# Output products one step earlier in PE's queue of the first feed-forward

## The chip, the cores and the metric

The kernel runs on one core of one Trainium2 chip. The metric is device time in microseconds, the median of several executions; lower is better. The profile shows one execution of its own. Engines: PE (TensorE) multiplies, ACT (ScalarE) and DVE (VectorE) read PE's results from the eight accumulator banks `ps`, POOL (GpSimd) works between SBUF tiles, SP issues most transfers.

## The reference

Two layers over 2048 tokens of width 128, each of them an attention and a feed-forward with eight experts, of which each token takes two. The change touches the feed-forward of the first layer:

```python
x = x + _L0_xattn_ref(_layernorm(x), ctx_1024, ctx_1024, ...)
x = x + _L0_ffn_ref(_layernorm(x), L0_ffn_w_gate, L0_ffn_w_g, L0_ffn_w_u, L0_ffn_w_d)
x = x + _L1_xattn_ref(_layernorm(x), ctx_1024, ctx_1024, ...)
x = x + _L1_ffn_ref(_layernorm(x), L1_ffn_gate_w, ...)

def _L0_ffn_ref(x, w_gate, w_g, w_u, w_d):      # D = 128, M = 176, E = 8, K = 2
    scores = x @ w_gate
    topk_scores, topk_idx = jax.lax.top_k(scores, K)
    topk_probs = jax.nn.softmax(topk_scores, axis=-1)
    gating = jnp.sum(jax.nn.one_hot(topk_idx, E) * topk_probs[..., None], axis=-2)
    hidden = jax.nn.silu(jnp.einsum('bsd,edm->ebsm', x, w_g)) * jnp.einsum('bsd,edm->ebsm', x, w_u)
    expert_out = jnp.einsum('ebsm,emd->ebsd', hidden, w_d)
    return jnp.einsum('bse,ebsd->bsd', gating, expert_out)
```

## The kernel before

Every engine has a program of its own, written out by hand in the order in which the engine issues it; semaphores join them. The stages are: loading and keys, values and queries of layer 0, attention 0, routing, the first feed-forward (`experts0` on each engine), and then the same for layer 1 with its own feed-forward (`experts1`).

A product in better than float16 precision is three products of a high and a low float16 part (helper `three`, lines 963 to 965: high by high, high by low, low by high). All products of the two feed-forwards have these three lines in the trace; the tile names tell them apart: `ps<-area,wg` and `ps<-area,wu` are gate and up, `ps<-wd,area` are the output products.

The first feed-forward treats the eight experts' hidden rows, 8 x 176 = 1408, as 11 blocks of 128 (STEPS0), and the tokens as four groups of 512. It has two halves (`i`), each with two groups: 22 steps (K0) in a half. Step k, n over both halves:

- PE, `gate_up(n)` (line 1191): six products of 512 columns, three for gate into bank k % 2 and three for up into bank 2 + k % 2. It waits until DVE has finished step n - 2 (semaphore `gt`), because the banks are reused. The first two steps of each half are issued ahead: those of half one in `routing`, those of half two in the tail of half one (line 1213).
- PE, line 1212: one product of 512 columns that spreads the tokens' expert weights over the hidden rows, into bank 4 + k % 2. It increments `up`.
- ACT, line 407: Silu of the gate bank, after `up`. Then, in ACT's queue, line 413: the float16 copy (`hid`, high part) of the step before, k - 1, after `gt` of that step. In four steps of a half (CHUNK_STEPS 2, 7, 12, 17) line 418 follows, a conversion of later weights.
- DVE, line 835: up times Silu; line 841: times the spread expert weights, into `gated`; it increments `gt`. DVE also makes the low parts of the later weights (line 847) and, after step 15, adds the first group's result to x with new statistics (`residual0`, lines 857 to 577); that of the second group comes after step 21.
- POOL, line 554: the low part of `hid`, `gated` minus the float16 copy; it increments `lo`. After step 16 POOL has the statistics of the first group as well (lines 495 and 498).
- PE, `down` (line 1172): twelve products of 128 columns, `hid` by the output weights, accumulated over the 11 steps of a group into bank 6 or 7. It waits for `lo` of its step. LAG0 = 3: it is issued three steps behind.

`hid`, `gated` and `act_f` have four buffers each.

Of the kernel before, what the change touches and what calls it, by code (L numbers as in the profile page):

```python
# [31 lines left out]
P = 128  # L32
# [14 lines left out]
STEPS0 = HID0 // P  # L47
# [9 lines left out]
def positive_wait(eng, sem, value):  # L57

    if not isinstance(value, int) or value > 0:
        eng.wait_ge(sem, value)  # L60


def build(nc, a, out):
# [5 lines left out]
    with ExitStack() as ctx:  # L69
        def sb(name, shape, dt):  # L70
            return ctx.enter_context(nc.sbuf_tensor(name, shape, dt))

        def sems(names, suffix=""):
            return {n: ctx.enter_context(nc.semaphore(n + suffix)) for n in names.split()}
# [46 lines left out]
        wd = sb("wd", [P, 2, HID0], F16)  # L121
# [11 lines left out]
        def carve(shape, dt):  # L133
            n = int(np.prod(shape)) * (4 if dt == F32 else 2) // 4
            ap = area[:, used[0]:used[0] + n]
            used[0] += n
            assert used[0] <= 12400, used
            if dt != F32:
                ap = ap.bitcast(dt)
            names = "abcd"[:len(shape)]  # L140
            if len(shape) > 1:
                ap = ap.rearrange(f"p ({' '.join(names)}) -> p {' '.join(names)}", **dict(zip(names[1:], shape[1:])))
            return ap
# [18 lines left out]
        hid = carve([4, 2, GT], F16)  # L162
# [16 lines left out]
        ps = ctx.enter_context(nc.psum_tensor("ps", [P, 8, 512], F32))  # L179
# [11 lines left out]
        F = [sems("xh xd xt_ps xt_hi xt_lo lg_ps lg top idx ex pr oh cb c16 ct_ps ct_a ct_d "  # L191
                  "up act hi lo down res " + ("t1 gt", "b1 b2_ps b2_r")[l], f"_f{l}") for l in range(2)]
# [767 lines left out]
        def _(pe):  # L960
            def three(dst, lhs, rhs, start=True, stop=True, **kw):

                pe.matmul(dst, lhs[0], rhs[0], start=start, stop=False, **kw)  # L963
                pe.matmul(dst, lhs[0], rhs[1], start=False, stop=False, **kw)  # L964
                return pe.matmul(dst, lhs[1], rhs[0], start=False, stop=stop, **kw)  # L965
# [208 lines left out]
            def down(dst, h, w, first, last):  # L1174


                for t in range(G):
                    r = slice(t * P, (t + 1) * P)
                    mm = three(dst[:, r], (h[:, 0, r], h[:, 1, r]), w, start=first and t == 0, stop=last, skip_group_check=True)
                return mm  # L1180

            K0 = 2 * STEPS0
            LAG0 = 3

            def place0(n):
                i, k = divmod(n, K0)
                f = slice((k % STEPS0) * P, (k % STEPS0 + 1) * P)
                tok = slice(1024 * i + GT * (k // STEPS0), 1024 * i + GT * (k // STEPS0) + GT)
                return i, k, f, tok

            def gate_up(n):

                i, k, f, tok = place0(n)
                xs = (xTa[:, 0, tok], xTa[:, 1, tok])
                positive_wait(pe, F[0]["gt"], n - 1)
                three(ps[:, k % 2, :], (wg[:, 0, f], wg[:, 1, f]), xs)
                three(ps[:, 2 + k % 2, :], (wu[:, 0, f], wu[:, 1, f]), xs)

            def experts0():
                q = F[0]  # L1200
                pe.wait_ge(q["ct_d"], 1)
                for i in range(GROUPS // 2):
                    for k in range(K0 + LAG0):
                        n = K0 * i + k
                        if k < K0:
                            _, _, f, tok = place0(n)
                            if k >= 2:
                                gate_up(n)
                            if n == K0:
                                pe.wait_ge(q["ct_a"], 1)  # L1210
                            positive_wait(pe, q["gt"], n - 1)
                            pe.matmul(ps[:, 4 + k % 2, :], expert_rows[:, f], combT[:, tok], start=True, stop=True).then_inc(q["up"], 1)  # L1212
                        elif i == 0 and k < K0 + 2:
                            gate_up(n)
                        if k >= LAG0:
                            j = k - LAG0
                            pe.wait_ge(q["lo"], K0 * i + (j + 1))
                            if j == 0:
                                pe.wait_ge(q["res"], 2 * i + 1)
                            half, f = divmod(j, STEPS0)  # L1220
                            down(ps[:, 6 + half, :], hid[:, j % 4, :, :],
                                 (wd[:, 0, f * P:(f + 1) * P], wd[:, 1, f * P:(f + 1) * P]), f == 0, f == STEPS0 - 1).then_inc(q["down"], 1)

            K1 = GROUPS * STEPS1
            LAG1 = 3
# [62 lines left out]
            attention(0)  # L1288
            routing(0)
            experts0()  # L1290
            for g in range(GROUPS):
                project_keys(1, g)
# [40 lines left out]
```

## Time and profile before

| | us |
|---|---|
| median of 3 runs (lowest, highest) | 533.04 (532.51, 534.41) |
| the profiled execution's own time | 533.98 |
| its span, first to last instruction | 531.8 |
| the first feed-forward on PE, from its first product of line 1212 to its last output product | 137.6 to 243.8 |
| PE busy in the span | 464.0 (87%) |
| DVE, ACT, POOL busy | 386.5, 368.3, 191.5 |
| mean granted clock of TensorE | 0.91 |

Shares of the whole span are means over stages with different limits, so the feed-forward is to be read from its own stretch. A granted clock of 1.00 is the 2.4 GHz level, 0.50 is 1.2 GHz; a value between them is a stretch with both. PE's matmuls overlap: a record lasts longer (0.38 us for 512 columns, 0.22 for 128) than the distance to the next start (0.215 and 0.056), so the beat is read from starts. In the rows, a time in brackets is the idle time of the engine before the instruction and what ended it. A step's number isn't printed; it is counted from the starts of line 1212, one in each step.

### The profile page before, as it was taken

What the parts mean: (1) busy time and instruction counts of PE and PEld (TensorE: products, weight loads), DVE (VectorE), ACT (ScalarE), POOL (GpSimd) and SP (SyncE); (2) the same over time, 40 slices, a digit from 0 to 9 for tenths busy, and PEclk for the clock granted to TensorE, in tenths of its full rate; (3) what the DMA queues carried; (4) which work ended last, traced back from release to release, by engine and by line L of the source; (5) the groups of instructions that cost most, each with busy time, mean ns of one, the idle gap of its engine ahead of it and who ended that gap; (6) DMA issues with size and microseconds to landing.
All of it is one profiled execution on the core that took longest, in us unless ns stands there. A gap on an engine that the chain in (4) does not pass through costs nothing.

```text
span 531.8 us, 15145 instructions
## 1 busy us (share of the span) xinstructions
PE 464.0 (87%) x5467; PEld 313.3 (59%) x5467; DVE 386.5 (73%) x1006; ACT 368.3 (69%) x675; POOL 191.5 (36%) x285
## 2 busy tenths in 40 slices
PE   5669888875899979994969999669999999999996
PEld 3445656553366536653636666537777777777775
DVE  6765888878587857784636999878767676676765
ACT  3555676771455536553837878548999999999995
POOL 7921576771155545566503887510000000000000
PEclk9895698995799989998867999859999999999999
DMA  7292000000012101100130000000000000000002
GB/s 188 49 280 54 2 3 1 3 2 1 0 41 76 46 2 39 41 1 9 19 56 1 3 4 1 4 1 2 1 2 1 0 0 0 0 0 0 0 21 59
DMA packets 18952, 13.47 MB, mean 25 GB/s; under 512 B 1682, under 2 KB 17236, under 8 KB 18900
## 3 DMA queue, kind: packets, MB, share of 16 engines
q1 hardware_dynamic: 18840, 12.75, 9.3%
q8 instruction: 34, 0.56, 0.5%
q14 instruction: 18, 0.15, 0.1%
q10 hardware_dynamic: 60, 0.02, 0.0%
HBM read 9.61 MB, written 1.05 MB: 20 GB/s over the span
## 4 chain that ended last, share of the span: by engine, by line
PE 58%; issue 12%; DVE 12%; POOL 9%; ACT 6%; DMA 1%; SPq 1%; POOLq 0%; DVEq 0%; ACTq 0%
PE ps L963 15%; PE ps L965 14%; PE ps L964 14%; POOL area L554 5%; PE ps L1117 4%; PE ps L1049 3%; DVE area L739 2%; PE ps L1076 2%; ACT vals L316 1%; PE ps L1007 1%; PE ps L1025 1%; DVE area L715 1%; POOL rstd L498 1%; POOL area L519 1%; DVE stats L573 1%
## 5 line engine op out<-in xcount | busy, mean ns | idle before, releaser
L892 DVE TENSOR_TENSOR area<-area 128x512 f16<-128x512 f32 x128 | 87.9, 689 | 46.4 <-ACT area L436 45.9
L963 PE MATMUL ps<-w,area 128*128 (+1 forms) x512 | 92.3, 219 | 0.5 <-DVE area L892 0.5
L964 PE MATMUL ps<-w,area 128*128 (+1 forms) x512 | 92.3, 219 | 0.0
L965 PE MATMUL ps<-w,area 128*128 (+1 forms) x512 | 92.3, 219 | 0.0
L432 ACT ACTIVATE area<-ps,b_now 128x512 f32<-128x512 f32 x128 | 87.7, 685 | 2.9 <-ACT b_now L426 1.3
L436 ACT ACTIVATE area<-area 128x512 f16<-128x512 f32 x128 | 80.6, 630 | 4.1
L554 POOL TENSOR_TENSOR area<-area 128x512 f16<-128x512 f32 x44 | 51.0, 1159 | 54.8 <-ACT area L413 54.8
L963 PEld LDWEIGHTS ps<-w,area 128*128 128x128 f16 x512 | 50.1, 98 | 15.3 <-DVE area L892 1.2
L964 PEld LDWEIGHTS ps<-w,area 128*128 128x128 f16 x512 | 50.1, 98 | 14.2
L739 DVE TENSOR_REDUCE area<-ps 128x8 f32<-128x512 f32 x64 | 41.2, 685 | 19.6 <-PE ps L1117 19.6
L407 ACT ACTIVATE area<-ps 128x512 f32<-128x512 f32 x44 | 26.0, 597 | 40.2 <-PE ps L1212 39.7
L965 PEld LDWEIGHTS ps<-w,area 128*128 128x128 f16 x512 | 50.1, 98 | 0.0
L963 PE MATMUL ps<-area,w 128*128 128x512 f16 x128 | 49.2, 385 | 0.8 <-DVE area L799 0.8
L964 PE MATMUL ps<-area,w 128*128 128x512 f16 x128 | 49.3, 385 | 0.0
L965 PE MATMUL ps<-area,w 128*128 128x512 f16 x128 | 49.3, 385 | 0.0
L1049 PE MATMUL ps<-ident,area 128*128 128x128 f32 x256 | 44.3, 323 | 0.2 <-ACT area L364 0.2
L835 DVE SCALAR_TENSOR_TENSOR area<-ps,area 128x512 f32<-128x512 f32 x44 | 30.2, 685 | 18.9 <-ACT area L407 18.7
L1117 PE MATMUL ps<-keys,q_T 32*64 32x256 f16 x768 | 39.5, 314 | 2.9 <-DVE q_T L673 1.6
L534 POOL TENSOR_TENSOR area<-area 128x512 f16<-128x512 f32 x32 | 41.4, 1293 | 0.1
L364 ACT ACTIVATE area<-ps 128x512 f32<-128x512 f32 x64 | 34.7, 594 | 5.6 <-PE ps L1076 4.6
L913 DVE SCALAR_TENSOR_TENSOR x_res<-ps,area,x_res 128x128 f32<-128x128 f32 x128 | 35.8, 343 | 0.9 <-PE ps L965 0.9
L1049 PEld LDWEIGHTS ps<-ident,area 128*128 128x128 f32 x256 | 33.6, 165 | 3.9 <-ACT area L364 1.8
(185 smaller groups left out, 1171.9 us busy)
## 6 DMA issues: line engine op xcount, KB each, us to landing
w_stage<-in_L_ffn_W SPq DMA_DIRECT2D x8, 512.0 KB, 4.1
keys<-area SPq DMA_DIRECT2D x32, 48.0 KB
area<-in_ctx SPq DMA_DIRECT2D x4, 256.0 KB, 4.0
x_res<-in_x SPq DMA_DIRECT2D x4, 256.0 KB, 5.3
out<-x_res SPq DMA_DIRECT2D x4, 256.0 KB, 2.3
w<-in_L_ffn_w_g SPq DMA_DIRECT2D x1, 704.0 KB, 4.5
w<-in_L_ffn_w_u SPq DMA_DIRECT2D x1, 704.0 KB, 6.3
w<-in_L_ffn_w_d SPq DMA_DIRECT2D x1, 704.0 KB, 8.2
```

The source lines that it names most:

```text
L432: nc.scalar.activation(act_f[:, k % 4, :], ps[:, k % 4, :], ACT.Gelu, bias=b1_now[:, k % STEPS1:k % STEPS1 + 1], scale=1 / WSCALE).then_in ...
L436: nc.scalar.activation(hid[:, k % 4, 0, :], act_f[:, k % 4, :], ACT.Copy).then_inc(q["hi"], 1)
L534: nc.gpsimd.tensor_tensor(pT[:, (t + 1) % 2, 1, 4:8, :].rearrange("p a b -> p (a b)"), p_f[:, (t + 1) % 2, :], pT[:, (t + 1) % 2, 0, 4:8, ...
L554: nc.gpsimd.tensor_tensor(hid[:, k % 4, 1, :], gated[:, k % 4, :], hid[:, k % 4, 0, :], ALU.subtract).then_inc(q["lo"], 1)
L739: nc.vector.tensor_reduce(mx[:, v, h * hh:(h + 1) * hh], ps[:, 2 * v + h, :].rearrange("p (h k) -> p h k", k=SEQ), axis=AX.X, op=ALU.max). ...
L892: nc.vector.tensor_tensor(hid[:, k % 4, 1, :], act_f[:, k % 4, :], hid[:, k % 4, 0, :], ALU.subtract).then_inc(q["lo"], 1)
L913: ins = nc.vector.scalar_tensor_tensor(x[:, G * g + t, :], ps[:, 4 + g % 2, t * P:(t + 1) * P], comb[:, G * g + t, bass.ds(e, 1)], x[:, G ...
L963: pe.matmul(dst, lhs[0], rhs[0], start=start, stop=False, **kw)
L964: pe.matmul(dst, lhs[0], rhs[1], start=False, stop=False, **kw)
L965: return pe.matmul(dst, lhs[1], rhs[0], start=False, stop=stop, **kw)
L1049: mm = pe.transpose(ps[:, 4 + h, n * P:(n + 1) * P], probs[:, (t + 1) % 2, c:c + P], ident[:, :])
L1117: mm = pe.matmul(ps[64 * b:64 * b + 64, 2 * v + n // 2, HALF // 2 * odd:HALF // 2 * (odd + 1)].rearrange("p (j k) -> p j k", j=QUAD), q_T[ ...
```

## The change

The output products become a function, `put_down(i, j)`, with the same waits in the same order and the same products. In steps 3 to 21 of a half it is called at the beginning of the step, ahead of `gate_up(n)` and of line 1212, and no longer behind them. In the three last turns (k from 22 to 24) `gate_up` of the next half is still issued first. LAG0 stays 3, and no other engine's program is changed.

```diff
@@ experts0 of PE
                         if k < K0:
                             _, _, f, tok = place0(n)
+                            if k >= LAG0:
+                                put_down(i, k - LAG0)
                             if k >= 2:
                                 gate_up(n)
                             if n == K0:
                                 pe.wait_ge(q["ct_a"], 1)
                             positive_wait(pe, q["gt"], n - 1)
                             pe.matmul(ps[:, 4 + k % 2, :], expert_rows[:, f], combT[:, tok], start=True, stop=True).then_inc(q["up"], 1)
-                        elif i == 0 and k < K0 + 2:
-                            gate_up(n)
-                        if k >= LAG0:
-                            j = k - LAG0
-                            pe.wait_ge(q["lo"], K0 * i + (j + 1))
-                            if j == 0:
-                                pe.wait_ge(q["res"], 2 * i + 1)
-                            half, f = divmod(j, STEPS0)
-                            down(ps[:, 6 + half, :], hid[:, j % 4, :, :],
-                                 (wd[:, 0, f * P:(f + 1) * P], wd[:, 1, f * P:(f + 1) * P]), f == 0, f == STEPS0 - 1).then_inc(q["down"], 1)
+                        else:
+                            if i == 0 and k < K0 + 2:
+                                gate_up(n)
+                            put_down(i, k - LAG0)
+
+            def put_down(i, j):
+
+                q = F[0]
+                pe.wait_ge(q["lo"], K0 * i + (j + 1))
+                if j == 0:
+                    pe.wait_ge(q["res"], 2 * i + 1)
+                half, f = divmod(j, STEPS0)
+                down(ps[:, 6 + half, :], hid[:, j % 4, :, :],
+                     (wd[:, 0, f * P:(f + 1) * P], wd[:, 1, f * P:(f + 1) * P]), f == 0, f == STEPS0 - 1).then_inc(q["down"], 1)
```

## Rows read from the trace of the kernel before

**Rows 1.** The stretches: us, each engine's busy us (instructions), TensorE clock, DMA share, GB/s.

```profile
203.00:225.00 22.00, 22.00 (x193) 13.62 (x192) 16.70 (x25) 13.05 (x22) 11.78 (x11) 1.00 0.16 48
```

**Rows 2.** The waits of 137 to 246 us: who waited for whom, us, times, longest.

```profile
PE ps L963 <- DVE area L841: 6.7, 4, 3.5
...
PE ps L963 <- POOL area L554: 1.9, 2, 1.1
```

**Rows 3.** The timeline, steps 10 to 12 of half two: start, us, engine.

```profile
214.28 0.22 PE L963 MATMUL ps<-wd,area 128*128 128x128 f16 x1
...
214.95 0.38 PE L963 MATMUL ps<-area,wg 128*128 128x512 f16 x1
...
216.25 0.38 PE L1212 MATMUL ps<-area,expert_rows 128*128 128x512 f16 x1
...
216.46 0.22 PE L963 MATMUL ps<-wd,area 128*128 128x128 f16 x1
...
217.16 0.62 ACT L413 ACTIVATE area<-area 128x512 f16<-128x512 f32 x1
...
217.85 1.16 POOL L554 TENSOR_TENSOR area<-area 128x512 f16<-128x512 f32 x1 [1.02 <-ACT area L413]
...
218.02 0.69 DVE L841 TENSOR_TENSOR area<-ps,area 128x512 f32<-128x512 f32 x1
...
218.43 0.38 PE L1212 MATMUL ps<-area,expert_rows 128*128 128x512 f16 x1
```

**Rows 4.** The timeline, end of half two: POOL's end and the products waiting for it.

```profile
240.37 1.16 POOL L554 TENSOR_TENSOR area<-area 128x512 f16<-128x512 f32 x1 [1.02 <-ACT area L413]
...
241.58 0.23 PE L963 MATMUL ps<-wd,area 128*128 128x128 f16 x1 [1.10 <-POOL area L554]
...
243.17 0.23 PE L963 MATMUL ps<-wd,area 128*128 128x128 f16 x1 [0.75 <-POOL area L554]
...
243.85 0.38 PE L963 MATMUL ps<-ctx_T,wT 128*128 128x512 f16 x1
```

**Rows 5.** The timeline, start of half one, steps 2 to 5.

```profile
142.81 0.59 PE L1212 MATMUL ps<-area,expert_rows 128*128 128x512 f16 x1
...
144.62 1.16 POOL L554 TENSOR_TENSOR area<-area 128x512 f16<-128x512 f32 x1 [2.51 <-ACT area L413]
...
149.07 0.38 PE L1212 MATMUL ps<-area,expert_rows 128*128 128x512 f16 x1
```

**Rows 6.** The timeline, steps 15 to 21 of half one, with the first residual.

```profile
170.88 0.38 PE L1212 MATMUL ps<-area,expert_rows 128*128 128x512 f16 x1
...
176.08 0.69 DVE L841 TENSOR_TENSOR area<-ps,area 128x512 f32<-128x512 f32 x1
...
177.51 1.16 POOL L554 TENSOR_TENSOR area<-area 128x512 f16<-128x512 f32 x1 [1.69 <-ACT area L413]
...
178.13 0.38 PE L1212 MATMUL ps<-area,expert_rows 128*128 128x512 f16 x1
...
180.22 1.16 POOL L554 TENSOR_TENSOR area<-area 128x512 f16<-128x512 f32 x1
```

**Rows 7.** The timeline, step 21 and the end of half one.

```profile
184.68 0.38 PE L1212 MATMUL ps<-area,expert_rows 128*128 128x512 f16 x1
...
187.88 1.16 POOL L554 TENSOR_TENSOR area<-area 128x512 f16<-128x512 f32 x1 [0.44 <-ACT area L413]
...
190.16 0.59 PE L1212 MATMUL ps<-area,expert_rows 128*128 128x512 f16 x2
```

**Rows 8.** The timeline, start of half two, steps 2 and 3.

```profile
196.74 0.63 PE L1212 MATMUL ps<-area,expert_rows 128*128 128x512 f16 x1
...
198.80 0.38 PE L1212 MATMUL ps<-area,expert_rows 128*128 128x512 f16 x1
```

**Rows 9.** The stretches in the two attention stages (columns as in Rows 1).

```profile
80.00:90.00 10.00, 8.76 (x131) 6.00 (x130) 7.98 (x22) 6.89 (x15) 6.87 (x12) 0.83 0.01 2
290.00:300.00 10.00, 9.36 (x157) 6.10 (x160) 9.20 (x28) 7.91 (x19) 7.75 (x15) 1.00 0.01 2
```

## Prediction

> **Names.** Step k is one of the 22 steps of a half (44 in the first feed-forward). G(k) are its six gate and up products (512 columns each), C(k) the product that spreads the expert weights, D(k) its twelve output products (128 columns each). S(k) is ACT's Silu, M(k) DVE's last multiplication, H(k) ACT's float16 copy, L(k) POOL's subtraction (L554), which D(k) waits for. Times "C(k) + 2.76" count from the start of C(k).
>
> **What bounds the kernel now.** I read first the stretches, to see which engine is full in the feed-forward: from 203 to 225 us PE is busy 22.00 of 22.00 us at a granted clock of 1.00, the 2.4 GHz level, while DVE, ACT and POOL are at 16.70, 13.05 and 11.78 [rows 1]. Second the waits: in the whole feed-forward the output products wait for POOL twice only, 1.9 us, and the gate products for DVE four times, 6.7 us [rows 2]. So POOL's result is always there in time, but for the end. The chain of waits names POOL L554 step after step here; that is how it walks back through ACT and PE's queue, and the full PE speaks against it. Third the timeline, for the beat: C(11) starts at 216.25 and C(12) at 218.43, 2.18 us apart [rows 3]. That is PE's own work: 214.28 to 214.95 for D (0.67), then to 216.25 for G (1.30), then 0.21 for C, 2.18 in all. PE issues without a hole.
>
> **The change, part by part.** No instruction is added or removed, and no DMA, SP, ACT, DVE or POOL instruction moves. In PE's queue each group C(k), D(k-3), G(k+1) becomes C(k), D(k-2), G(k+1): between two G the output products are those of one step later. So the real edit is a lag of 2 in place of 3, and D's wait is now in front of G(k+1), C(k+1) and all behind them, and through C(k+1) in front of S, M, H and L of that step.
>
> *When L is ready.* With C(11) at 216.25, H(10) starts at 217.16 (it is queued behind S(11), which needs C(11)), L(10) runs 217.85 to 219.01 [rows 3]. So L(k-1) ends at C(k) + 2.76. M(11) ends at 218.71, C(11) + 2.46, before ACT comes to H(11) a beat later (217.16 + 2.18 = 219.34): M is not the late one. Before, D(k-1) is reached after C(k+2), at C(k) + 4.57, 1.8 us after L; that is the cover. After, it is reached after C(k+1), at C(k) + 2.18 + 0.21 = 2.39, and L is 0.37 us late.
>
> *What a waiting D costs.* At the end of half two L ends at 240.37 + 1.16 = 241.53 and the waiting product starts at 241.58: 0.05 from one to the other. A D that has waited takes 243.17 to 243.85, 0.68 [rows 4], then 1.30 for G: 1.98 to the next C.
>
> *The loop.* C(k+2) = C(k) + 2.76 + 0.05 + 1.98 = C(k) + 4.79, in place of 2 x 2.18 = 4.36. One wait of 0.43 in every two steps (or smaller ones that come to it), since a late C(k+2) pushes its own S, H and L, and gives the D in between its time back: 0.215 us a step. From step 5 to 15 of each half that is 10 x 0.215 = **2.15 us**, twice. The bounds: with no cost on restarting (0.05 and 0.01 left out) 4.73, or 0.185 a step; with ACT's hand-over to POOL, 217.16 + 0.62 = 217.78 to 217.85, 0.07 in place of 0.05 [rows 3], 0.225. A wait of 0.42 in every step, 2.60 a beat, is excluded, as the D in between finds its L ready. I take the row that shows the very wait.
>
> *The start of half one.* C(2) stands at 142.81 as before; C(2) takes 0.43 at the low clock; D(0) is ready, so it goes in at 143.24, and C(3) comes at 143.24 + 0.67 + 1.30 = 145.21. L(1) ends at 144.62 + 1.16 = 145.78 [rows 5], so D(1) at 145.83, C(4) at 147.81. L(2) ends at C(3) + 2.76 = 147.97, D(2) at 148.02, C(5) at 150.00 against 149.07: **+0.93**, of which 0.67 is only the D done earlier. *Of half two:* C(2) at 196.74 at a low clock; D(0) behind it, half of it at the low level (0.33 more): C(3) at 196.74 + 0.43 + 1.00 + 1.30 = 199.47, in place of 198.80 [rows 8]. In half one L(1) ends 144.62 + 1.16 - 142.81 = 2.97 after C(2) [rows 5]; here that is 199.71, D(1) at 199.76 and C(4) at 201.74. L(2) ends at 199.47 + 2.76 = 202.23, so D(2) at 202.28, C(5) at 204.26. Before it is 216.25 - 6 x 2.18 = 203.17 [rows 3]: **+1.09**. A low stretch can end elsewhere: 0.7 either way.
>
> *Steps 15 to 21, with the first residual on DVE.* Before, M(16) ends at 176.77, C(15) + 5.89, as DVE does the residual first; that makes PE wait and puts C(18) at 178.13, C(15) + 7.25, of which 0.71 is over three beats [rows 6]. The loop's own three steps come to about 7.19, so the new wait hides in the old one: C(18) at +7.25 to 7.39. After that L(16), 177.51 to 178.67, M(16) + 1.90, gives D(16) at +7.84 and C(19) at +9.82. L(17) stands behind POOL's own statistics, starts at 180.22 and ends at 181.38, M(16) + 4.61 [rows 6], so D(17) starts at +10.55 and C(20) at +12.53; D(18) is ready when reached, C(21) at +14.71. Before: 184.68 - 170.88 = 13.80 [rows 6, 7]. **+0.91**, in each half.
>
> *The end of a half.* The tail keeps its order, with one D less in it (D(18) is done). In half one before, C(22) starts at 190.16, C(21) + 5.48, all PE work. After, PE would be 0.67 earlier, but L(21) ends at 187.88 + 1.16 = 189.04, C(21) + 4.36 [rows 7]; D(21) starts at +4.41, C(22) 0.68 later at +5.09, or +5.12 with a small wait of G for M(21): **-0.36**. In half two D(21) waits for L(21) before and after: **0**, and nothing is paid back.
>
> *Sum.* Half one 0.93 + 2.15 + 0.91 - 0.36 = 3.63, half two 1.09 + 2.15 + 0.91 = 4.15: +7.8 us. Nothing later hides it: DVE's second residual, POOL's normalisation and the key transfers all start from the end of half two. Against the profiled run: 531.8 + 7.8 = 539.6 of span, with the 2.2 around it 541.8. The median of the runs shown, 533.04, is 0.94 below the profiled run, 533.98. I forecast **540.8**.
>
> **Rivals.** *Not slower.* The loop decides at one point: L(k-1) has to end by C(k) + 2.34, and it ends at 2.76. If the rows put PE's starts 0.4 too early against POOL's (matmul ends are modelled), or H went ahead of S, there is no wait, and what is left are gains: the early D fills PE's wait of 0.71 at the residual in both halves, and 0.36 at the tail: 533.0 - 1.8 = 531.3. For it: the margin is a sixth of a beat. Against it: the 0.05 between POOL and PE is read from the same two clocks, and the two waits at the end of half two are real ones [rows 4]. Chance 0.05.
>
> *The clock falls.* PE, full until now, gets a hole in every second step. In the first attention, where PE waits for others, a stretch has 8.76 of 10 us busy and a granted clock of 0.83 (a part of it at the 1.2 GHz level), but in the second one 9.36 busy goes with 1.00 [rows 9]; after the change PE would be busy about 91%. At 0.83 a pair of steps is 4.36 / 0.83 = 5.25 of PE work, 0.46 over the 4.79 of the forecast; over the 16 pairs of steps 5 to 21 of both halves that is +7.4, 548.2. Chance 0.06.
> The Trainium skill ("TensorE: Matmul & The Clock Gate", A second HAM failure mode: psum-queue depth-cycling) says that frequent micro-idles between groups of matmuls can make the clock go to and fro between its levels; by it the result would be this rival. The row of the second attention stage disagrees, that of the first fits.
>
> *Something unseen*: 0.04.
>
> **How the numbers follow.** The forecast has 0.85. Its own bounds: 0.03 less a step or 0.01 more, over 32 steps, is -1.0 or +0.3; the starts 0.7 each; the low stretches of the later stages, which can fall elsewhere when all is 7.8 us later, 1.5. Not all go one way: 538.0 to 544.0. The rivals at 531.3 and 548.2 stay outside with 0.11. A measurement of this kernel tells some 0.5% (2.7 us) from no change: slower by more 0.94, within 0.03, faster by more 0.03 (a gain of 1.8 is still "within").
>
> **What the profile would show.** The waits of the feed-forward should have a new large group, PE's output products for POOL L554, about 16 to 25 times at some 0.26 each (0.21 + 0.43 after the start of C, less the 0.38 that C's record lasts), while PE's wait for DVE before step 18 goes to near nothing. The starts of C should be about 2.4 apart on average, uneven (2.18 and 2.6), POOL's subtractions as well, all durations unchanged, the granted clock 1.00 in the steady stretches. The feed-forward should end near 251.6 in place of 243.85, and what follows keep its length. Even beats of 2.18 would prove the first rival, a clock under 1.00 in a steady stretch the second. I am wrong in size if ACT turns H ahead of S, or if the starts of the halves hide more than I think.

## The result, and the profile after

| | before | after |
|---|---|---|
| median of 5 runs, us (lowest, highest) | 533.91 (532.51, 534.41) | 540.63 (539.67, 541.84) |
| the profiled execution's own time | 533.98 | 539.67 |
| its span | 531.8 | 537.5 |
| PE from its first product of the first feed-forward (C(0)) to the first product behind it | 137.56 to 243.85 = 106.3 | 138.98 to 252.09 = 113.1 |

The ratio of after to before is 1.0134, 95% interval 1.0113 to 1.0155: 6.7 us slower. The forecast was 540.8.

The waits of after, from 137 to 254 us (who waited for whom, us in total, times, longest), answer to [rows 2]:

```profile
PEld ps L963 <- POOL area L554: 23.3, 40, 1.5
...
PE ps L963 <- DVE area L841: 5.6, 2, 3.5
...
PE ps L963 <- POOL area L554: 5.2, 15, 1.3
```

PE's output products now wait for POOL, and not only at the end: 15 times with 5.2 us, of which the two waits at the end of half two are 1.34 and 0.75. That leaves 13 of 0.24 each. The row of the weight loads (PEld), 40 times against 2 before, shows that nearly every D has to wait; many of these waits don't appear on the matmul row, because the record of C lasts 0.38 us and covers them. The wait for DVE went from four times to two: the two of 0.5 us at the residual are off the matmul row. The large ones, up to 3.5 us at the starts of the halves, are still there.

The timeline of after, steps 7 to 10 of half two (start, us, engine), answers to [rows 3]:

```profile
216.43 0.62 ACT L413 ACTIVATE area<-area 128x512 f16<-128x512 f32 x1
...
217.13 1.16 POOL L554 TENSOR_TENSOR area<-area 128x512 f16<-128x512 f32 x1 [1.26 <-ACT area L413]
...
217.90 0.38 PE L1214 MATMUL ps<-area,expert_rows 128*128 128x512 f16 x1
...
218.34 0.23 PE L963 MATMUL ps<-wd,area 128*128 128x128 f16 x1
...
219.02 0.38 PE L963 MATMUL ps<-area,wg 128*128 128x512 f16 x1
...
219.51 1.16 POOL L554 TENSOR_TENSOR area<-area 128x512 f16<-128x512 f32 x1 [1.22 <-ACT area L413]
...
220.32 0.38 PE L1214 MATMUL ps<-area,expert_rows 128*128 128x512 f16 x1
...
220.72 0.23 PE L963 MATMUL ps<-wd,area 128*128 128x128 f16 x1
```

H(7) at 216.43 and L(7) from 217.13 to 218.29 stand behind S(8), as before. But D(7) is now what PE has next after C(9), at 217.90 + 0.21 = 218.11, and it starts at 218.34, 0.05 after the end of L(7). G(10) follows at 219.02, C(10) at 220.32. One beat later D(8) has its turn at 220.53 and starts at 220.72, again 0.05 after L(8) (219.51 + 1.16 = 220.67). Two steps take 4.80 us. In half two the wait is spread over both steps (2.42 and 2.38), in half one it falls mostly on every other (2.57 and 2.22). The sum is the same.

The clock, in stretches of the steady part of each half (columns as in [rows 1]):

```profile
149.00:173.00 24.00, 22.89 (x194) 12.74 (x191) 16.73 (x25) 13.07 (x23) 11.58 (x10) 1.00 0.15 46
...
203.00:225.00 22.00, 21.59 (x175) 11.64 (x173) 15.96 (x23) 11.60 (x20) 10.84 (x10) 1.00 0.17 48
```

It is 1.00 in both, so the holes did not bring it down. PE is busy 22.89 of 24 us by its records, which cover part of each hole; the holes themselves are 0.44 in 4.80.

### The profile page after: what moved, and what is told of

Read it like the earlier page. It is cut to its first block, busy times and chain, and to the rows that moved or that the text cites. A ratio compares the mean times of both kernels' runs of the same rounds, so it can differ in the third digit from the quotient of the medians.

```text
span 537.5 us, 15145 instructions
## 1 busy us (share of the span) xinstructions
PE 465.6 (87%) x5467; PEld 309.5 (58%) x5467; DVE 388.9 (72%) x1006; ACT 368.6 (69%) x675; POOL 191.1 (36%) x285
## 3 DMA queue, kind: packets, MB, share of 16 engines
HBM read 9.61 MB, written 1.05 MB: 20 GB/s over the span
## 4 chain that ended last, share of the span: by engine, by line
PE 50%; issue 19%; POOL 12%; DVE 11%; ACT 5%; DMA 1%; SPq 1%; POOLq 1%; DVEq 0%; ACTq 0%
PE ps L963 12%; PE ps L965 12%; PE ps L964 12%; POOL area L554 8%; PE ps L1117 4%; PE ps L1049 3%; DVE area L739 2%; PE ps L1076 2%; ACT vals L316 1%; PE ps L1025 1%; DVE area L715 1%; PE ps L1007 1%; POOL rstd L498 1%; DVE stats L573 1%; DMA x_res<-in_x 1%
## 5 line engine op out<-in xcount | busy, mean ns | idle before, releaser
L963 PE MATMUL ps<-wd,area 128*128 128x128 f16 x176 | 32.3, 222 | 5.9 <-POOL area L554 5.2
```

## The steps of the forecast, one by one

From the starts of C in both profiles (of each pair the second is after), us:

| stretch | half one | difference, forecast | half two | difference, forecast |
|---|---|---|---|---|
| C(0) to C(2) | 5.25, 4.02 | -1.23, 0 | 6.58, 6.66 | +0.08, 0 |
| C(2) to C(5) | 6.26, 7.36 | +1.10, +0.93 | 6.42, 7.43 | +1.01, +1.09 |
| C(5) to C(15) | 21.81, 24.00 | +2.19, +2.15 | 21.81, 23.98 | +2.17, +2.15 |
| C(15) to C(21) | 13.80, 14.69 | +0.89, +0.91 | 13.79, 14.70 | +0.91, +0.91 |
| C(21) to the next stretch | 5.48, 5.17 | -0.31, -0.36 | 5.09, 5.10 | +0.01, 0 |

The last row of half two ends at the first product behind the feed-forward. The sum is +6.8, or +8.05 without the first cell; the forecast was +7.8. Outside the feed-forward, what stands before it was 1.4 longer in this execution and what stands behind it 2.5 shorter.

The first cell isn't the change's doing. C(0) to C(2) takes 5.25 us in six of the fourteen kernels profiled here and 4.02 in the other eight, in both orders, and C(2) itself starts at 142.81 before and 143.00 after. The +1.10 beside it is also made up otherwise than the forecast had it. It took D(0) to be ready behind C(2); but L(0) ended at 142.38 + 1.15 = 143.53, and D(0) waited for it, to 143.59. In the run with a lag of two (below), where C(0) to C(2) is 5.25 as before, C(2) to C(5) takes 7.19 us, +0.93, as reckoned.

Two rows need their lines. Steps 15 to 18 of half one, which answer to [rows 6] (C(15), M(16), C(18)):

```profile
174.36 0.38 PE L1214 MATMUL ps<-area,expert_rows 128*128 128x512 f16 x1
...
179.55 0.69 DVE L841 TENSOR_TENSOR area<-ps,area 128x512 f32<-128x512 f32 x1
...
181.61 0.38 PE L1214 MATMUL ps<-area,expert_rows 128*128 128x512 f16 x1
```

C(15) to C(18) is 7.25 as before: M(16) still ends 5.88 after C(15) and sets G(18). What the loop costs in these three steps hides in the wait for M(16), and the whole +0.9 of the stretch comes behind C(18), from the waits of D(16) and D(17). The end of half one, which answers to [rows 7]:

```profile
189.05 0.38 PE L1214 MATMUL ps<-area,expert_rows 128*128 128x512 f16 x1
...
191.57 0.39 PE L963 MATMUL ps<-area,wg 128*128 128x512 f16 x1
...
192.26 1.15 POOL L554 TENSOR_TENSOR area<-area 128x512 f16<-128x512 f32 x1 [0.43 <-ACT area L413]
...
194.22 0.59 PE L1214 MATMUL ps<-area,expert_rows 128*128 128x512 f16 x2
```

C(21) starts at 189.05, G(23) at 191.57, and C(22) with C(23) at 194.22, 5.17 later. L(21) ends at 192.26 + 1.15 = 193.41, while PE comes to D(21) only at 191.57 + 1.30 + 0.67 = 193.54 (G(23), D(20)). So the tail is not set by L(21), which the forecast made its first bound (5.09), but by M(21), which ends at C(21) + 2.46 = 191.51 and lets G(23) begin. The forecast had that as "a small wait of G for M(21)", 5.12.

## The experiments

Each was compared with the kernel before, run beside it on the same chip (medians 533.92, 533.96 and 533.64 for the three groups of four). Stretches are read from the starts of C in the profile, as above.

**One half only.** In half one the order of the change, in half two that of before.

```diff
-                            if k >= LAG0:
+                            if k >= LAG0 and i == 0:
                                 put_down(i, k - LAG0)
                             if k >= 2:
                                 gate_up(n)
...
                             pe.matmul(ps[:, 4 + k % 2, :], ...).then_inc(q["up"], 1)
+                            if k >= LAG0 and i == 1:
+                                put_down(i, k - LAG0)
```

> The output products stand ahead of the gate products in half one only; half two has the order of before. Theory (a loop of 4.79 us for two steps instead of 4.36, and the prices of the starts, the residual and the tails): half one costs 3.6 us and half two nothing, 537.5 us against 533.9 of before, ratio 1.0068. In the profile the steps 5 to 15 take 24.0 us in half one and 21.8 in half two. Rival (the clock, or anything that concerns the whole program, makes the difference): the two halves look alike, or the later stages differ, and the time lies near 534 or near 541.

Measured: 538.82 us, ratio 1.0086 (1.0056 to 1.0115). The profiled execution has C(5) and C(15) of half one, then of half two, at

```profile
151.93 0.38 PE L1214 MATMUL ps<-area,expert_rows 128*128 128x512 f16 x1
...
175.92 0.38 PE L1214 MATMUL ps<-area,expert_rows 128*128 128x512 f16 x1
...
208.75 0.38 PE L1214 MATMUL ps<-area,expert_rows 128*128 128x512 f16 x1
...
230.56 0.38 PE L1214 MATMUL ps<-area,expert_rows 128*128 128x512 f16 x1
```

so 23.99 us in half one and 21.81 in half two. The residual stretch is 14.70 and 13.79. The loss goes with the order, half by half; nothing that concerns the whole program explains it. The time is 4.9 us over before, 1.3 more than forecast; the forecast ratio, 1.0068, is inside the interval, and both 1 and the 1.0134 of the change are outside.

**A lag of two, in the place of before.** The one line of LAG0 in the kernel before.

```diff
-            LAG0 = 3
+            LAG0 = 2
```

> The order of before, with LAG0 at 2 instead of 3: C(k), D(k-2), G(k+1), with D still written behind G and C of its step. Theory (the change is nothing but a lag of 2): the steps 5 to 15 take 24.0 us in both halves, C every 2.4 us on average, and the time is that of the changed kernel within 1 us, 540 to 541.5 us, ratio 1.012 to 1.015. Rival (the place ahead of G matters by itself, as the weights for G can't be loaded while D waits): D now waits in the same place of the stream, so this rival would have to give something else than the changed kernel, and under 1.005 if the lag were harmless.

Measured: 540.58 us, ratio 1.0126 (1.0067 to 1.0184), beside 540.63 of the changed kernel. Steps 5 to 15 take 24.00 and 23.99 us, 15 to 21 14.70 and 14.69. The timeline of half two (start, us, engine):

```profile
212.17 0.38 PE L1212 MATMUL ps<-area,expert_rows 128*128 128x512 f16 x1
...
212.81 0.23 PE L963 MATMUL ps<-wd,area 128*128 128x128 f16 x1 [0.26 <-POOL area L554]
...
213.78 1.16 POOL L554 TENSOR_TENSOR area<-area 128x512 f16<-128x512 f32 x1 [1.02 <-ACT area L413]
...
214.79 0.38 PE L1212 MATMUL ps<-area,expert_rows 128*128 128x512 f16 x1
```

C(k) at 212.17, C(k+1) at 214.79, 2.62 later, and then 2.18; D starts at 212.81, not at 212.38. Written as a move ahead of the gate products, the change is a shorter lag. In the steps of a half both kernels give PE the same row of products, so this run shows that the two are one change. It can't show whether the place of the wait ahead of G costs anything by itself; the next run and the one with a shorter L do that, as they keep the place and take the wait away.

**High part first, in the changed order.** The wait for L stands before the last four products of D.

```diff
+            def down_high_first(dst, h, w, first, last, j):
+                for t in range(G):
+                    r = slice(t * P, (t + 1) * P)
+                    pe.matmul(dst[:, r], h[:, 0, r], w[0], start=first and t == 0, stop=False, ...)
+                    pe.matmul(dst[:, r], h[:, 0, r], w[1], start=False, stop=False, ...)
+                pe.wait_ge(F[0]["lo"], j)
+                for t in range(G):
+                    r = slice(t * P, (t + 1) * P)
+                    mm = pe.matmul(dst[:, r], h[:, 1, r], w[0], start=False, stop=last, ...)
+                return mm
...
-                pe.wait_ge(q["lo"], K0 * i + (j + 1))
+                pe.wait_ge(q["hi"], K0 * i + (j + 1))
...
-                down(ps[:, 6 + half, :], ...
+                down_high_first(ps[:, 6 + half, :], ...
```

> The changed kernel, with D in two parts: the eight products with the high part of hid first, behind a wait for ACT's copy H only, then the wait for POOL's L and the four products with the low part. L is needed 8 x 0.056 = 0.45 us later, 2.84 after C instead of 2.39, and it is there at 2.81. Theory (the loss is L coming 0.42 us too late and nothing else): C every 2.18 us in the steady steps, steps 5 to 15 take 21.8 us; what is left is the start of each half (+0.67), D(17) behind POOL's statistics (+0.46) and a gain at the tails (-0.6 and -0.45): 535 us, ratio 1.002. Rival (holes or the order on PE itself, or the clock): it stays at 1.010 or more.

Measured: 534.36 us, ratio 1.0012 (0.9981 to 1.0044). Steps 5 to 15 take 21.81 us in both halves. L of POOL, C, the first product of D, the first with the low part (four in one row), the next C:

```profile
210.77 1.16 POOL L554 TENSOR_TENSOR area<-area 128x512 f16<-128x512 f32 x1 [1.02 <-ACT area L413]
...
211.34 0.38 PE L1226 MATMUL ps<-area,expert_rows 128*128 128x512 f16 x1
...
211.56 0.22 PE L1186 MATMUL ps<-wd,area 128*128 128x128 f16 x1
...
212.00 0.39 PE L1191 MATMUL ps<-wd,area 128*128 128x128 f16 x4
...
213.52 0.38 PE L1226 MATMUL ps<-area,expert_rows 128*128 128x512 f16 x1
```

L ends at 211.93, 0.37 too late for the first product of D at 211.56, and 0.07 ahead of the first product with the low part at 212.00. The beat is 2.18 again. The instructions are the same on all engines; D alone has its products in two parts and its wait between them, and the loss in the steady steps is gone: the cause is that L comes late, and by how much. What is left is in part as forecast: 15 to 21 takes 14.26 (L(17) behind POOL's statistics, +0.46), and the end of half two 4.64 in place of 5.09 (-0.45). C(2) to C(5) is +0.28 and +1.05, where +0.67 each was expected. The tail of half one missed: 5.16, 0.3 shorter than before and not 0.6. With L out of the way, this shows again that M(21) sets it. C(15) to C(18) is still 7.25.

**High part first, in the order of before.** The same edit of D in the kernel before.

> Control of the run before: the order of before, with D in the same two parts. Theory: L is 1.8 us early in every step, so the steady steps stay at 2.18; only the last D of half two, which waits for L, is 0.45 us shorter: 533.5 us, ratio 0.999. Rival (the two parts gain or cost something by themselves, for instance at the loading of weights): a ratio under 0.996 or over 1.004 here, by which the run before would have to be read anew.

Measured: 534.52 us, ratio 0.9996 (0.9964 to 1.0027); all steady stretches as before, 21.81 and 13.80, and the end of half two 4.65 in place of 5.09, as expected. In the time of the whole kernel the edit has neither a price nor a gain that could be measured.

**A longer L, both orders.** One subtraction of 192 columns more, ahead of L.

```diff
                     pool.wait_ge(q["hi"], n + 1)
+                    nc.gpsimd.tensor_tensor(hid[:, k % 4, 1, 0:192], gated[:, k % 4, 0:192],
+                                            hid[:, k % 4, 0, 0:192], ALU.subtract).then_inc(q["pd"], 1)
+                    pool.wait_ge(q["pd"], n + 1)
                     nc.gpsimd.tensor_tensor(hid[:, k % 4, 1, :], gated[:, k % 4, :], hid[:, k % 4, 0, :],
                                             ALU.subtract).then_inc(q["lo"], 1)
```

> The order of before, with one more POOL subtraction of 192 columns ahead of each L (192 of its 512 columns are done twice), which L waits for: L ends about 0.6 us later, at C + 3.4. Theory (in the order of before D has 1.8 us of cover): the steady steps stay at 2.18 us, only the tails lose, 0.2 in half one and 0.6 in half two: 534.7 us, ratio 1.0015. Rival (POOL's pace or its traffic costs time by itself): over 1.005.

> The changed order with the same 0.6 us more ahead of L. Theory (two steps take L's latency + 0.05 + 1.98): 4.79 + 0.6 = 5.4 us for two steps, 2.7 a step in place of 2.4, so that steps 5 to 15 take 27 us in place of 24; with the starts, the residual part and the tails about 12 us more than the changed kernel: 552.5 us, ratio to before 1.035. Rival (the wait is paid in every step): 0.6 a step, 44 steps, 26 us more, 566 us. Rival (POOL's result isn't what D waits for): no more than with the order of before.

Measured in the order of before: 537.48 us, ratio 1.0065 (1.0034 to 1.0097). The ten steady steps lose only 0.21 and 0.29 us for ten times 0.62 of longer L: the cover of 1.8 us holds. The forecast of the total missed, and by its number the rival (over 1.005) came true. In the profile the feed-forward loses 4.5 us from C(2) on. Some 2.7 of it, in steps 15 to 21 and in the tails, is L coming late where its cover is thin. The first such place is D(17), behind POOL's statistics (the two POOL rows are the added piece and L(17)):

```profile
182.28 1.09 POOL L554 TENSOR_TENSOR area<-area 128x192 f16<-128x192 f32 x1
...
183.45 1.16 POOL L557 TENSOR_TENSOR area<-area 128x512 f16<-128x512 f32 x1
...
184.66 0.23 PE L966 MATMUL ps<-wd,area 128*128 128x128 f16 x1 [0.56 <-POOL area L557]
```

L(17) ends at 184.61 and D(17) waits 0.56; the added piece took 1.09 here, not 0.55. Steps 15 to 21 take 14.56 in place of 13.80, in both halves, the tails 0.4 and 0.8 more, C(2) to C(5) 0.6 and 0.7. I had put 0.2 and 0.6 on the tails and nothing on the two other places.

The rest, in the steady steps and the starts, goes with the rival, a price of POOL's work by itself. DVE's conversion of later weights in step 7 of half one, in the kernel before:

```profile
156.16 0.69 DVE L847 SCALAR_TENSOR_TENSOR w<-w_stage,w 128x512 f32 x1 [0.27 <-ACT w L418]
```

and here, with L(6) ahead of it:

```profile
156.67 1.16 POOL L557 TENSOR_TENSOR area<-area 128x512 f16<-128x512 f32 x1
...
157.16 1.21 DVE L850 SCALAR_TENSOR_TENSOR w<-w_stage,w 128x512 f32 x1 [0.27 <-ACT w L418]
```

The conversion takes 1.21 in place of 0.69 where POOL's subtraction runs into it, up to 157.83, and ends 0.54 behind it. DVE's next multiplications come late by it, and the beats from C(9) and C(14) are 2.27 and not 2.18. At the start of half one a conversion takes 1.27, and PE waits 0.46 us for DVE at 148.75, in the beat from C(4).

In the order of the change: 557.3 us, ratio 1.0431 (1.0385 to 1.0478). Steps 5 to 15 take 27.12 us in both halves, 5.42 for two steps. The added piece, L, C, D, the next C:

```profile
220.12 0.55 POOL L554 TENSOR_TENSOR area<-area 128x192 f16<-128x192 f32 x1 [1.27 <-ACT area L413]
...
220.74 1.15 POOL L557 TENSOR_TENSOR area<-area 128x512 f16<-128x512 f32 x1
...
220.88 0.38 PE L1217 MATMUL ps<-area,expert_rows 128*128 128x512 f16 x1
...
221.95 0.23 PE L966 MATMUL ps<-wd,area 128*128 128x128 f16 x1 [0.70 <-POOL area L557]
...
223.93 0.38 PE L1217 MATMUL ps<-area,expert_rows 128*128 128x512 f16 x1
```

L starts 0.62 later (220.12 to 220.74), and D starts 0.06 after its end (221.89 to 221.95). 4.79 + 0.62 = 5.41 against 5.42: the formula of the loop, with its slope of one half a step, and not the rival's 0.6 in every step, which would be 3.0 a step where 2.71 is measured. Steps 15 to 21 take 16.93 in place of 14.70, and from C(2) to the first product behind the feed-forward it is 13.0 us more than in the changed kernel, where about 12 was expected. The total is 4.8 over its forecast, which lies outside the interval (1.035 for 1.0385 to 1.0478). The profile doesn't show the rest: the execution that was profiled took 553.26 us, 0.8 over the forecast, and was the fastest of four; why the other three took 556.4 to 558.3 stays open.

**A shorter L, in the changed order.**

```diff
+                    c = GT if k < 4 else GT // 2
-                    nc.gpsimd.tensor_tensor(hid[:, k % 4, 1, :], gated[:, k % 4, :], hid[:, k % 4, 0, :],
+                    nc.gpsimd.tensor_tensor(hid[:, k % 4, 1, 0:c], gated[:, k % 4, 0:c], hid[:, k % 4, 0, 0:c],
                                             ALU.subtract).then_inc(q["lo"], 1)
```

> The changed order, with POOL's subtraction cut to 256 of 512 columns from step 4 of each half on; the low part of the other columns is left as an earlier step put it, so this kernel leaves out half of that subtraction. L ends about 0.48 us earlier, at C + 2.28, and the point from which there is no wait is 2.34. Theory: steady steps at 2.18 us, the rest is the starts and the tails: 535 us, ratio 1.002. Rival (the change costs by something else than L's end): 1.010 or more.

Measured: 535.72 us, ratio 1.0026 (1.0000 to 1.0052). Steps 5 to 15 take 21.85 and 21.81:

```profile
211.60 0.67 POOL L555 TENSOR_TENSOR area<-area 128x256 f16<-128x256 f32 x1 [1.51 <-ACT area L413]
...
212.17 0.38 PE L1215 MATMUL ps<-area,expert_rows 128*128 128x512 f16 x1
...
214.35 0.38 PE L1215 MATMUL ps<-area,expert_rows 128*128 128x512 f16 x1
```

L takes 0.67 and ends at 212.27; PE comes to D at 212.17 + 0.21 = 212.38. With L ending at C + 2.28 there is no wait, at 2.76 there is: the deciding point, 2.34, lies between. The starts keep their price (C(2) to C(5) is 7.4 and 7.7), as L has its full length in steps 0 to 3 and one D more stands ahead of C(3). L at 0.67, 1.16 and 0.62 + 1.16 thus gives 21.8, 24.0 and 27.1 us for the ten steps.

**Two lags.** Lag 3 to step 16, two D in step 17 in PE's hole, lag 2 from there, high part first, POOL's statistics three steps later.

```diff
+                        if k < 17:
+                            js = [k - 3] if k >= 3 else []
+                        elif k == 17:
+                            js = [14, 15]
+                        elif k < K0:
+                            js = [k - 2]
+                        else:
+                            js = [k - 2] if k < K0 + 2 else []
...
-                    if k == STEPS0 + 5:
+                    if k == STEPS0 + 8:
                         rstds(8 * i, G, 8 * i + 2 * TILES)
```

> A version meant to be faster than both: a lag of 3 up to step 16, in step 17 two D (14 and 15) where PE would wait 0.71 us for DVE's residual, and a lag of 2 from there, with D in two parts (high first) and POOL's statistics of the first group moved three steps later, behind L(19). Theory: no wait for L in the steady steps; one D of 0.67 fills the hole at step 18, which shortens PE's tail of half one by 0.6, and the last D of half two is 0.45 shorter: 532.9 us, ratio 0.998. Rival (a lag of 2 costs by itself): slower than before, by 5 steps of 0.2 in each half, 1.004.

Measured: 532.35 us, ratio 0.9975 (0.9944 to 1.0007), not told apart from before. Steps 15 to 21 take 13.80, so the second D was free, but the tail of half one is 5.34 in place of the 4.9 expected. The statistics, moved, now stand before L(20) (the second row is L(20) and L(21)), and D(20) waits for it:

```profile
184.02 1.01 POOL L498 TENSOR_TENSOR rstd<-mean_var,minus_half 128x4 f32 x1 [0.21 <-POOL mean_var L495]
...
185.00 2.43 POOL L554 TENSOR_TENSOR area<-area 128x512 f16<-128x512 f32 x2
...
186.21 0.40 PE L1191 MATMUL ps<-wd,area 128*128 128x128 f16 x4 [0.35 <-POOL area L554]
```

**One run of 44 steps.** PE is full in the steady steps, so a gain has to come from the holes: 12.06 us from C(21) to C(24) of the next half where 6.54 would do, and 0.71 at each residual. ACT, DVE, POOL and PE go through steps 0 to 43 without a break, buffers by n % 4, DVE's residual is cut in three, and POOL's statistics come one step later.

```diff
-                for i in range(GROUPS // 2):
-                    for k in range(K0 + LAG0):
+                for n in range(4 * STEPS0 + LAG0):
...
-                        if k == STEPS0 + 4:
-                            residual0(i, 0)
-                    residual0(i, 1)
+                        if n > STEPS0:
+                            residual0(n // STEPS0 - 1, n % STEPS0)
...
-                    if k == STEPS0 + 5:
-                        rstds(8 * i, G, 8 * i + 2 * TILES)
+                if n > STEPS0 and n % STEPS0 == 6:
+                    rstds(G * (n // STEPS0 - 1), G, G * (n // STEPS0 - 1) + 2 * TILES)
```

> A version built on what the rows show: PE is full in the steady steps, so what can be won lies in the holes. The 44 steps are one run on every engine, with the lag of 3 and the products of before: steps 22 and 23 are no longer issued behind a tail, and DVE's residual of a token group is split over three steps (the addition after step 14, the statistics after 15, their end after 16, counted from the group's first step), so that each piece fits DVE's 0.76 us of slack. Theory: from C(21) to C(24) 6.5 us in place of 12.06, so 5.5 less; the two waits of 0.71 at the residual go, 1.4 less: 527 us, ratio 0.987, C every 2.18 us from the fifth step to the last. Rival (DVE can't take the pieces, or POOL's statistics come in the way): holes at steps 16 to 19 remain, 529 us.

Measured: **527.01 us, ratio 0.9872 (0.9844 to 0.9900)**, faster than both kernels, 6.6 us below before. C(21) to C(24) takes 6.54 us. From 150 to 232 us of its span (columns as in [rows 1]):

```profile
150.00:232.00 82.00, 82.00 (x718) 50.93 (x716) 67.84 (x123) 49.09 (x83) 47.92 (x44) 1.00 0.13 40
```

PE is busy all of 82 us at a clock of 1.00. DVE, at 67.84, has taken the residuals in. As a record lasts longer than the distance to the next start, 82.00 doesn't exclude small holes: two beats are 2.24 and 2.34. PE's waits in the feed-forward are those of the start and the end:

```profile
PE ps L964 <- DVE area L839: 2.1, 1, 2.1
...
PE ps L964 <- POOL area L553: 1.8, 2, 1.1
```

> The same with the residual in one piece after step 15 (4 of the next group), as before: it tells the two gains apart. Theory: a hole of 0.71 at each of three residuals: 2.1 us more than the run before, 529 us, ratio 0.991. Rival (the pieces bring nothing): the same time as the run before.

Measured: 528.93 us, ratio 0.9897 (0.9876 to 0.9918). The beat is 2.80 in place of 2.18 at each of three residuals (0.62, where 0.71 was expected), 1.9 us together, which is the difference of the two medians. POOL's statistics also stand one step earlier here than in the run before. The intervals of the two overlap; the beats in the profiles don't.

> The one run of 44 steps with LAG0 at 2, which is the order of the change in a feed-forward without holes in it. Theory (a loop of 4.79 us for two steps, whatever stands around it): 0.215 a step over about 40 steps, 8.6 us more than with the lag of 3: 535.6 us, and 47.9 us for any 20 steady steps against 43.6. Rival (a large part of the change's cost came from the starts and tails): 4 us more or less.

Measured: 536.05 us, ratio 1.0040 (1.0026 to 1.0055), 9.0 us over the run with the lag of 3. Steps 5 to 15 take 23.98 us, as in the changed kernel. Twenty steps, C(5) to C(25), take 48.26 us against 43.62, the beats 2.18 and 2.61 in turn, but for one of 2.88 behind POOL's statistics (three of them in the run). The cost of the lag in the steady steps is the same whatever stands around it. In all, 9.0 us is more than the 6.6 us that the one run had won, so that the kernel with both is slower than before.

> The one run with a lag of 3 and D in two parts, the high part first. Theory: L has its cover in the steady steps, only the last D, which waits for L, is 0.45 us shorter: 526.6 us. Rival (D in two parts is dearer by itself): slower than the run with D as before by 1 us or more.

Measured: 526.23 us, ratio 0.9848 (0.9820 to 0.9876), the lowest of all, though 0.8 us less than the one run as it was is inside their intervals. In the profile four products follow the last wait instead of twelve: C(43) to the first product behind the feed-forward is 4.65, against 5.09 in the run with the residual in one piece, the 0.45 expected. (In the profile of the first of these runs it is 5.61, as its last D ran at a granted clock of 0.57.)

## Why the forecast was right, and where it was not

The step that carried it, the loop, holds to 0.01: 4.79 us for two steps forecast, 4.80 measured, 4.4 us of the 6.8 in the feed-forward. The experiments make it more than a number: L's length was changed both ways in this order, and the ten steps took 21.8, 24.0 and 27.1 us. It rested on three rows: when L ends after C, how long PE takes to start when released, and how long D and G last. The clock rival didn't come, the other one neither.

What went otherwise:

- That 540.8 lies 0.2 from the median 540.63 is luck. It was 533.04 + 7.8. Five runs of before give 533.91, and the difference is 6.7: a base 0.87 too low and a step 1.1 too large cancel. The feed-forward alone, from C(2) on, came out at +8.05.
- "All durations unchanged" didn't hold on DVE: its second weight conversion of a step pair (L847), 0.83 us before in the steady steps, takes 0.88 to 0.94 after, as it meets POOL's subtraction for longer. PE's ten steps took 24.00 and 23.98 where the loop gives 23.95, so it cost next to nothing.
- The tail of half one is set by M(21) and G(23), not by L(21). The size was right by chance (-0.31 for -0.36).
- The rival "not slower" was priced wrong. It had the early D filling PE's hole of 0.71 at the residual. With L out of the way (high part first, in the changed order) C(15) to C(18) is still 7.25: the change puts another D in front of G(18), not one more. It also left out the starts, where one D more ahead of C(3) delays each half by 0.67. The kernel with the shorter L is this rival made real but for the first four steps of a half, and took 535.7 us, not 531.3. Where one more D was really put into the hole, with two lags, it was free.
- The number of waits on the matmul row, 13 of 0.24 us behind the start and before the end, lies below the "16 to 25 times at some 0.26"; nearly all D wait, but where the 0.43 is spread over two steps each part hides behind C's record.
- The starts of stretches at a low clock had been given 0.7 each; the first one made 1.23, and the later stages, given 1.5, made 2.5. They go the same way here, and the 7.8 of the forecast was 5.7 in the spans of the two profiled executions. The medians are 6.7 apart.

The last point can be seen. The start of the feed-forward and two stretches of the second layer, before:

```profile
137.00:149.00 12.00, 9.55 (x57) 4.48 (x55) 7.80 (x14) 6.81 (x11) 4.03 (x4) 0.86 0.01 2
...
278.25:288.95 10.70, 10.34 (x123) 6.45 (x120) 5.25 (x11) 6.89 (x15) 3.07 (x6) 0.61 0.01 2
...
354.25:363.05 8.80, 7.89 (x61) 4.63 (x60) 6.13 (x17) 7.73 (x13) 0.00 (x0) 0.77 0.01 2
```

and after, the later two cut so that they hold the same work, within one product:

```profile
137.00:149.00 12.00, 9.13 (x78) 5.00 (x77) 7.94 (x14) 6.60 (x11) 3.46 (x3) 1.00 0.00 1
...
286.30:295.20 8.90, 7.89 (x123) 4.68 (x120) 5.25 (x11) 6.79 (x15) 3.06 (x6) 0.95 0.01 2
...
360.50:368.70 8.20, 6.91 (x60) 3.91 (x59) 6.04 (x17) 7.76 (x13) 0.00 (x0) 0.89 0.01 2
```

The granted clock is 0.86, 0.61 and 0.77 in the one, 1.00, 0.95 and 0.89 in the other, and the same 123 products take 10.70 and 8.90 us. These two later stretches hold 1.8 and 0.6 of the 2.5 us; PE's starts keep their distance from one profile to the other in all that follows the second.

In the fourteen profiles the time from the first product behind the feed-forward to the end of the span is 287.2 to 287.9 us in ten and 285.2 to 286.0 in four. The four are the changed kernel, the lag of two and the longer L in both orders, all of them kernels in which PE waits for POOL in the last steps of a half as well. So part of the 2.5 us can be an effect of the change and not of chance. The one run with a lag of two has such waits too, though, and is among the ten, and there is one profile of each kernel: what decides it isn't shown.

## What to carry to other kernels

Before moving work forward in an engine's queue, read the lag in the new order: what comes between the producer's release and the consumer now, and how long the way round is (here 2.76 us through ACT and POOL, from the start of the next step's C, while PE came to D after 2.39). If the way round is longer than what the engine has to do meanwhile, every step pays half of the excess where the wait feeds back after two steps, and the busy shares didn't show it beforehand (POOL's was 11.78 of 22 us). Look for gains where the full engine has holes, here at the seam of two halves and at the residual: closing them brought 1.3%.

## What the runs showed of the hardware

- From POOL's last column to the waiting product on PE 0.05 to 0.06 us passed, in every wait that was read. POOL's subtraction took 0.55, 0.67 and 1.16 us for 192, 256 and 512 columns: 1.9 ns a column and 0.18.
- POOL's subtraction and DVE's float32 weight conversion (L847, SBUF to SBUF) slowed each other where they met. A conversion takes 0.69 us alone. Where a subtraction still ran for 0.28 us or more behind its start, it took 0.83 to 1.56 and ended 0.54 or 0.55 behind the end of the subtraction each time, before, after and with the longer L. The other way round, a subtraction of 192 columns that started together with a conversion of 0.68 took 1.09 in place of 0.55.
- Holes of 0.4 us in every second step, or of 1.0 in the changed order with the longer L (a granted clock of 1.00 from 160 to 180 and from 215 to 240 us there), did not bring the granted clock down in the steady steps. The rule of the Trainium skill cited in the forecast ("TensorE: Matmul & The Clock Gate", A second HAM failure mode: psum-queue depth-cycling) did not show here: the trace disagrees, with 1.00.
- Where the low clock falls is worth up to 2.5 us in a span of 530, without a change in the work concerned. It sets how small a difference a profile pair can tell; the steps 5 to 15, read from starts at a clock of 1.00, took 21.81 us in ten of the eleven halves in which PE had no wait there (21.85 in the other), and 23.98 to 24.00 in the five with the order of the change or a lag of two, in the kernels of two halves without the longer L.
